# Who issues the transfers: weight and row loads from SyncE instead of GpSimd, stores from ScalarE

## The chip, the cores and the metric

The kernel runs on one core of a Trainium2 chip. The metric is the time of one execution on the device in microseconds (us), median of three runs. The core has TensorE (PE), VectorE (DVE), ScalarE (ACT), GpSimd (POOL) and SyncE (SP), and 16 DMA engines that move data between the chip's memory (HBM) and the on-chip memory.

## What is computed

For each of 128 samples the kernel adds to `x` (64 x 256, float32) its product with one of 64 weight matrices (256 x 256), chosen by the sample's category, and that category's bias:

```python
selected_W = W[cat_ids]
selected_b = b[cat_ids]
out = x + jnp.einsum('bsd,bdh->bsh', x, selected_W) + selected_b[:, None, :]
```

`x` is 8.4 MB, the result as much, a weight matrix 256 KB. With these inputs 54 of the 64 categories occur.

## The kernel before

**Plan.** From the categories the kernel first works out, on DVE and PE, a list of the categories in order of first use, so that each weight matrix is loaded once, into place n of `w_all`; "load n" below is the n-th of this list (0 to 63, of which 54 to 63 don't occur and are skipped by a condition). The list lies in `load_words`, four 6-bit categories to a 32-bit word; the issuing engine reads a word and takes a category out of it with shifts (`words_read` L162, `part` L166). A second list, `slot_words`, tells for each sample the place of its weights.

**Groups.** Samples are handled in 16 groups of 8, a group being four pairs. Rows of a group (512 KB) are loaded into one of ten slots of `rows` (`load_rows` L178). For each group PE transposes the rows of the *next* group (`transpose_half` L462, L464), writes the bias sums (L538), and does four pairs of products (L552). The weights of a sample are copied from `w_all` to `w_slot`, of even samples by DVE and of odd ones by ACT (`copy_weights` L298, L304); a copy waits until as many loads are reported as its place needs (L303), and until the pair that used the slot is done. ACT also copies the transposed rows from PSUM (`x_half` L309, L316). DVE adds the sums to the rows in place (`add_rows` L432, L433), two pairs at a time, and in groups 1 to 3 splits the bias (L419 to L427). Then the rows are stored.

Group 0 needs loads 0 to 7, group 1 up to 13, group 2 up to 19, group 3 up to 25, group 4 up to 31, and so on with fewer new ones: group 5 up to 32, 6 up to 37, 7 up to 40, 8 up to 43, 9 up to 46, 10 up to 47, 11 up to 51, 12 to 14 up to 52, 15 up to 53.

**Who issues what.** SyncE loads the categories, rows 0 to 2 and the bias, then loads 1, 3, 5, 7; ACT loads 0, 2, 4, 6. After that SyncE only reports: it waits for each load in order and adds one to `w_loads_done` (L211 to L217). GpSimd issues loads 8 to 63 (L260 to L279, `load_weights` L169, L170), beginning when three loads are reported (L263), with at most eight of them in flight (L274). Behind fixed loads it also issues the rows of groups 3 to 15 (`X_AFTER_LOAD` L37, L285) and the stores of groups 0 to 6 (`STORE_AFTER_LOAD` L38, L288); rows of group 10 and up wait until the store that frees their slot has landed. After the last load it stores groups 7 to 10 (L289). SyncE stores groups 11 to 14 in halves (L183) and two pairs of group 15 (L191), ACT the other two.

Transfers issued by GpSimd run on a queue that the profile calls software_dynamic (q0); those of SyncE and ACT on hardware_dynamic ones (q1 and q10).

Of the kernel before, what the change touches and what calls it, by code (L numbers as in the profile page):

```python
# [12 lines left out]
GROUP = 8  # L13
QUAD = 4
# [5 lines left out]
LOADS_IN_FLIGHT = 8  # L20
FIRST_X = 3
FIRST_LOADS = 8
REPORTED_FIRST = 3
CERTAIN_LOADS = 40
# [10 lines left out]


X_AFTER_LOAD = {3: 13, 4: 19, 5: 25, 6: 31, 7: 33, 8: 37, 9: 40, 10: 43, 11: 46, 12: 48, 13: 51, 14: 55, 15: 60}  # L37
STORE_AFTER_LOAD = {0: 37, 1: 40, 2: 43, 3: 46, 4: 48, 5: 51, 6: 59}  # L38
POOL_GROUPS = 11


def build_cond_residual(nc, x, cat, weights, bias, out):
# [18 lines left out]
    assert FIRST_LOADS % WORD == 0  # L61
    assert all(at + 1 >= min(C, GROUP * (g + 1) + QUAD - 1) for g, at in STORE_AFTER_LOAD.items())
    assert all(X_AFTER_LOAD[g + X_SLOTS] >= STORE_AFTER_LOAD[g] for g in range(GROUPS - X_SLOTS))

# [5 lines left out]
    with ExitStack() as ctx:  # L70
# [91 lines left out]
        def words_read(engine, words, most):  # L162

            return nc.values_load_multi_w_load_instructions(words, engines=[engine], min_val=0, max_val=most)[1]  # L164

        def part(word, n):  # L166
            return (word >> (BITS * n)) & (C - 1)

# [9 lines left out]
        def load_rows(engine, g):  # L178
            engine.dma_start(rows[:, g % X_SLOTS, :, :], x_groups[g]).then_inc(x_loaded[g], 16)  # L179
# [6 lines left out]
        def store_group(engine, g):  # L186
            engine.dma_start(out_groups[g], rows[:, g % X_SLOTS, :, :]).then_inc(stored[g % X_SLOTS], 16)  # L187
# [8 lines left out]
        @block.sync  # L196
        def _(sp):
            sp.dma_start(cats_i[:, :], cat.rearrange("(a b) -> a b", a=1)).then_inc(cats_loaded, 16)
            load_rows(sp, 0)
            sp.dma_start(bias_nat[:, :], bias).then_inc(bias_loaded, 16)  # L200
            for g in range(1, FIRST_X):
                load_rows(sp, g)

            sp.wait_ge(plan_read, 1)
            for n in range(1, FIRST_LOADS, PAIR):
                if n % WORD == 1:

                    word = words_read(mybir.EngineType.SP, load_words[0:1, n // WORD:n // WORD + 1],
                                      2 ** (WORD * BITS) - 1)[0]
                load_weights(sp, n, part(word, n % WORD))  # L210
            for n in range(C):  # L211

                if n < FIRST_LOADS:
                    sp.wait_ge(first_w_loaded[n], 16)
                else:
                    sp.wait_ge(w_loaded[n % LOADS_IN_FLIGHT], 16 * ((n - FIRST_LOADS) // LOADS_IN_FLIGHT + 1))
                sp.sem_inc(w_loads_done, 1)  # L217
            for q in range(QUADS_IN_GROUP * POOL_GROUPS, last_group):

                sp.wait_ge(sums_added, q + 1)  # L220
                store_quad(sp, q, late_stored)
            for p in range(0, PAIRS_IN_GROUP, PAIR):

                sp.wait_ge(sums_added, last_group + p + 1)
                store_pair(sp, p, last_stored)

            for g in range(POOL_GROUPS - X_SLOTS, POOL_GROUPS):
                sp.wait_ge(stored[g % X_SLOTS], stores_until(g))
            sp.wait_ge(late_stored, 16 * (last_group - QUADS_IN_GROUP * POOL_GROUPS))
            sp.wait_ge(last_stored, 16 * PAIRS_IN_GROUP)  # L230

        @block.gpsimd
        def _(pool):
# [16 lines left out]
                      allow_small_or_imprecise_dtypes=True).then_inc(consts_ready, 1)  # L250
            def store_sums(g):

                pool.wait_ge(sums_added, QUADS_IN_GROUP * (g + 1))
                store_group(pool, g)

            def list_word(w):
                return words_read(mybir.EngineType.Pool, load_words[0:1, w:w + 1], 2 ** (WORD * BITS) - 1)[0]


            pool.wait_ge(plan_read, 1)  # L260
            word = list_word(FIRST_LOADS // WORD)

            pool.wait_ge(w_loads_done, REPORTED_FIRST)  # L263
            for n in range(FIRST_LOADS, C):
                if n % WORD == 0 and n > FIRST_LOADS:
                    word = next_word
                if n % WORD == WORD - 1 and n + 1 < C:

                    next_word = list_word(n // WORD + 1)
                if n == CERTAIN_LOADS:  # L270
                    loads = words_read(mybir.EngineType.Pool, load_words[0:1, LIST_WORDS:LIST_WORDS + 1], C)[0]
                if n >= FIRST_LOADS + LOADS_IN_FLIGHT:

                    pool.wait_ge(w_loads_done, n - LOADS_IN_FLIGHT + 1)  # L274
                if n >= CERTAIN_LOADS:

                    load_weights(pool, n, part(word, n % WORD), cond=loads > n)
                else:
                    load_weights(pool, n, part(word, n % WORD))  # L279
                for g, after in X_AFTER_LOAD.items():  # L280
                    if after == n:
                        if g >= X_SLOTS:

                            pool.wait_ge(stored[g % X_SLOTS], stores_until(g - X_SLOTS))
                        load_rows(pool, g)  # L285
                for g, after in STORE_AFTER_LOAD.items():
                    if after == n:
                        store_sums(g)  # L288
            for g in range(len(STORE_AFTER_LOAD), POOL_GROUPS):  # L289
                store_sums(g)  # L290

# [16 lines left out]
        def _(act):  # L308
# [14 lines left out]
            act.wait_ge(cats_loaded, 16)  # L323
            load_weights(act, 0, words_read(mybir.EngineType.Activation, cats_i[0:1, 0:1], C - 1)[0])

            act.wait_ge(plan_read, 1)
# [10 lines left out]
            for g in range(GROUPS):  # L337
                if g >= 1:
                    for k in range(K):
                        x_half(g, k)  # L340

                now = slots
                if g + 1 < GROUPS:
                    slots = slots_of(mybir.EngineType.Activation, g + 1, 1)
                for p in range(PAIRS_IN_GROUP):
                    copy_weights(act, nc.scalar.copy, now[p], g, p, 1, odd_weights_ready)
            for p in range(1, PAIRS_IN_GROUP, PAIR):

                act.wait_ge(sums_added, last_group + p + 1)
                store_pair(act, p, last_stored)  # L350
# [108 lines left out]
        def _(pe):  # L459
# [22 lines left out]
            for n in range(WORD):  # L482
                T.matmul(load_words_ps, cat_powers[:, n:n + 1], has_place[:, n::WORD],
                         start=(n == 0), stop=(n == WORD - 1))
            T.matmul(loads_ps, is_first[:, :], ones[:, :], start=True, stop=True).then_inc(plan_products, 1)
            pe.wait_ge(plan_step, PLAN_STEPS["slots"])
            for n in range(WORD):
# [8 lines left out]

            pe.wait_ge(x_loaded[0], 16)
            for k in range(K):
                transpose_half(0, k)
            def group(g):  # L500
# [79 lines left out]
```

## Time and profile before

| | |
|---|---|
| median of three runs | 101.41 us (101.09 to 101.49) |
| the profiled execution | 101.62 us |
| its span (first to last record) | 99.9 us |
| granted TensorE clock, mean | 0.997 of full |
| busy: PE, DVE, ACT, POOL | 88%, 58%, 56%, 54% |
| moved by DMA | 31.19 MB, mean 312 GB/s |

All times inside the execution are counted from the span's start. The time of an execution holds the span and 1.7 us around it. A transfer's landing is when its semaphore is complete; loads count as available to the copies when SyncE has reported them.

### The profile page before, as it was taken

The page shows a single profiled execution, that of the slowest core. Times are in us where ns is not written, and L with a number is a line of the kernel's source. Part 1 is how long each engine was busy: PE and PEld are TensorE (multiplying, and loading weights), DVE is VectorE, ACT ScalarE, POOL GpSimd, SP SyncE. Part 2 cuts the span into 40 slices and gives each one's busy share as a digit, 9 for nine tenths or more (in the row PEclk, how much of TensorE's full clock was granted, in tenths as well). Part 3 has the DMA queues.
Part 4 walks back from the last instruction along what each step waited for, and adds up shares of the span by engine and source line. Part 5 has one row for each costly group of instructions (what it writes and reads, how often), then busy time and mean ns, then how long its engine had stood idle before and what let it go on. Part 6 is the DMA issues. An engine that isn't in the chain of part 4 may idle for free.

```text
span 99.9 us, 3043 instructions
## 1 busy us (share of the span) xinstructions
PE 87.6 (88%) x788; PEld 58.0 (58%) x788; DVE 58.4 (58%) x139; ACT 55.7 (56%) x98; POOL 53.8 (54%) x91
## 2 busy tenths in 40 slices
PE   0279559995699999899999999999999999999990
PEld 0148336753366667476767676666676767676640
DVE  2757126415989688864747484847373737373840
ACT  6004239363263565697848484858585858585500
POOL 5100088798799799988858755794333650000000
PEclk9999999999999999999999999999999999999998
DMA  0899988899999999999999999999998899993363
GB/s 0 268 322 366 349 223 285 297 298 362 318 323 354 354 353 336 354 348 346 390 374 390 366 397 372 398 387 385 380 369 300 272 337 337 343 302 105 105 210 108
DMA packets 13747, 31.19 MB, mean 312 GB/s; under 512 B 1505, under 2 KB 7714, under 8 KB 13730
## 3 DMA queue, kind: packets, MB, share of 16 engines
q0 software_dynamic: 7136, 24.65, 69.9%
q1 hardware_dynamic: 5218, 5.05, 15.4%
q10 hardware_dynamic: 1376, 1.31, 3.9%
q8 instruction: 6, 0.10, 0.4%
q14 instruction: 11, 0.09, 0.3%
HBM read 25.23 MB, written 8.39 MB: 336 GB/s over the span
## 4 chain that ended last, share of the span: by engine, by line
PE 56%; DMA 26%; issue 7%; POOL 2%; DVE 2%; POOLq 2%; SPq 1%; ACT 1%; ACTq 0%; DVEq 0%
PE mm_ps L552 37%; DMA w_all<-in_L_cond_W 25%; PE xt_ps L464 10%; PE mm_ps L538 6%; POOL w_all L170 2%; PE xt_ps L552 2%; DMA cats_i<-in_itok_B 1%; POOLq L170 1%; POOLq L164 1%; SPq L164 1%; ACT w_slot L304 1%; DVE rows L433 0%; POOL rows L179 0%; DVE same_ahead L381 0%; PE mm_ps L476 0%
## 5 line engine op out<-in xcount | busy, mean ns | idle before, releaser
L552 PE MATMUL mm_ps<-w_slot,xT 128*64 128x256 f32 x496 | 57.6, 380 | 3.7 <-DVE w_slot L304 1.9
L304 ACT COPY w_slot<-w_all 128x512 f32 x64 | 38.7, 619 | 31.7 <-SPq L217 20.9
L552 PEld LDWEIGHTS mm_ps<-w_slot,xT 128*64 128x64 f32 x496 | 34.4, 137 | 21.4 <-DVE w_slot L304 5.5
L170 POOL DMA_DIRECT2D w_all<-in_L_cond_W x56 | 33.8, 606 | 20.7 <-SPq L217 13.4
L433 DVE TENSOR_TENSOR rows<-mm_ps,rows 128x512 f32<-128x512 f32 (+1 forms) x32 | 21.5, 673 | 22.9 <-PE mm_ps L552 22.6
L304 DVE COPY w_slot<-w_all 128x512 f32 x64 | 27.7, 463 | 10.2 <-SPq L217 10.1
L316 ACT COPY xT<-xt_ps 128x512 f32<-128x512 f32 x32 | 17.2, 584 | 5.9 <-PE xt_ps L464 5.9
L464 PE MATMUL xt_ps<-ident,rows 128*128 128x128 f32 x128 | 19.1, 298 | 0.0
L464 PEld LDWEIGHTS xt_ps<-ident,rows 128*128 128x128 f32 x128 | 15.1, 151 | 6.4 <-issue 5.3
L179 POOL DMA_DIRECT2D rows<-in_x x13 | 10.1, 780 | 4.7 <-DMA out<-rows 3.3
L538 PE MATMUL mm_ps<-bias_parts,is_sample 96*64 96x256 bf16 x124 | 9.9, 278 | 0.0
L187 POOL DMA_DIRECT2D out<-rows x11 | 8.4, 769 | 1.1 <-issue 0.6
L538 PEld LDWEIGHTS mm_ps<-bias_parts,is_sample 96*64 96x64 bf16 x124 | 5.6, 109 | 3.3 <-issue 3.2
L470 PE MATMUL mm_ps<-bias_nat,in_category 64*96 64x256 f32 x8 | 3.1, 479 | 1.2 <-DVE rows L433 1.0
L422 DVE CAST bias_parts<-mm_ps 96x256 bf16<-96x256 f32 x4 | 1.7, 420 | 2.1 <-PE mm_ps L470 1.2
L476 PE MATMUL mm_ps<-cats,ones_row 1*128 1x128 bf16 x1 | 0.3, 283 | 2.7 <-DVE cats L373 2.7
L470 PEld LDWEIGHTS mm_ps<-bias_nat,in_category 64*96 64x96 f32 x8 | 1.1, 182 | 1.9 <-issue 1.5
L552 PE MATMUL xt_ps<-w_slot,xT 128*64 128x256 f32 x16 | 2.1, 379 | 0.0
L321 ACT ACT_TABLE_LOAD x1 | 1.3, 1283 | 0.9 <-PEq L569 0.9
L423 DVE TENSOR_TENSOR bias_rest<-mm_ps,bias_parts 96x256 f32<-96x256 f32 x4 | 1.7, 420 | 0.1
L426 DVE TENSOR_TENSOR bias_parts<-bias_rest,bias_mid 32x256 bf16<-32x256 f32 x4 | 1.7, 417 | 0.1
L476 PEld LDWEIGHTS mm_ps<-cats,ones_row 1*128 1x128 bf16 x1 | 0.1, 99 | 2.7 <-DVE cats L373 2.7
(46 smaller groups left out, 13.2 us busy)
## 6 DMA issues: line engine op xcount, KB each, us to landing
w_all<-in_L_cond_W POOLq DMA_DIRECT2D x56, 256.0 KB
rows<-in_x POOLq DMA_DIRECT2D x13, 512.0 KB, 7.0
out<-rows POOLq DMA_DIRECT2D x11, 512.0 KB, 7.6
out<-rows SPq DMA_DIRECT2D x8, 256.0 KB, 3.7
rows<-in_x SPq DMA_DIRECT2D x3, 512.0 KB, 6.5
w_all<-in_L_cond_W ACTq DMA_DIRECT2D x4, 256.0 KB, 5.7
w_all<-in_L_cond_W SPq DMA_DIRECT2D x4, 256.0 KB, 6.4
out<-rows SPq DMA_DIRECT2D x2, 128.0 KB, 1.7
```

Source lines behind the costliest of these rows:

```text
L164: return nc.values_load_multi_w_load_instructions(words, engines=[engine], min_val=0, max_val=most)[1]
L170: engine.dma_start(w_all[:, n, :, :], weights[bass.ds(c, 1), :, :].rearrange("c (k p) h -> p (c k) h", p=P), **how).then_inc(first_w_loade ...
L179: engine.dma_start(rows[:, g % X_SLOTS, :, :], x_groups[g]).then_inc(x_loaded[g], 16)
L187: engine.dma_start(out_groups[g], rows[:, g % X_SLOTS, :, :]).then_inc(stored[g % X_SLOTS], 16)
L304: copy(w_slot[:, PAIR * p + half, :, :].rearrange("p k h -> p (k h)"), w_all[:, bass.ds(c, 1), :, :].rearrange("p c k h -> p (c k h)")).th ...
L316: nc.scalar.copy(xT[:, slot, k].rearrange("p j s -> p (j s)"), xt_ps[slot][k][:, :, :].rearrange("p t r -> p (t r)")).then_inc(xT_ready, 1)
L422: split(V.tensor_copy(bias_parts[all3, t, :], whole))
L433: V.tensor_tensor(to, sums, to, ALU.add).then_inc(sums_added, 1)
L464: last = T.transpose(xt_ps[g % XT_SLOTS][k][:, p, :], rows[:, g % X_SLOTS, p, k * P:(k + 1) * P], ident[:, :])
L470: return T.matmul(bias_ps[t], in_category[:, t, :, :].rearrange("c a n -> c (a n)"), bias_nat[:, :], start=True, stop=True)
L538: T.matmul(sums(pair)[HALF * half:HALF * (half + 1), :], is_sample[:, sample + half:sample + half + 1].broadcast_to([ROWS, HALF]), bias_pa ...
L552: last = T.matmul(to[HALF * half:HALF * (half + 1), :], xT[:, slot, k, j, :], w_slot[:, j, k, :], start=False, stop=(k == K - 1), skip_gro ...
```

## The change

SyncE issues loads 8 to 63 right behind its own first ones, and the rows of groups 1 and 3 to 15; it reads each word of the list when it needs it. GpSimd, after making its constants, only reports. ACT issues rows 2 behind load 0, and stores groups 0 to 9, each behind its copies of a fixed later group (`STORED_IN_GROUP`); it has a wait for the sums first, of groups whose sums are older. Group 10 is now stored by SyncE in halves. In the first stage PE transposes group 0's rows before it packs the slot words, and ACT copies group 1's transposed rows between its first weight copies. The rows of groups 11, 13, 14 and 15 are issued after a later load than before.

```diff
-FIRST_X = 3
-REPORTED_FIRST = 3
-X_AFTER_LOAD = {3: 13, 4: 19, 5: 25, 6: 31, 7: 33, 8: 37, 9: 40, 10: 43, 11: 46, 12: 48, 13: 51, 14: 55, 15: 60}
-STORE_AFTER_LOAD = {0: 37, 1: 40, 2: 43, 3: 46, 4: 48, 5: 51, 6: 59}
-POOL_GROUPS = 11
+X_AFTER_LOAD = {3: 13, 4: 19, 5: 25, 6: 31, 7: 33, 8: 37, 9: 40, 10: 43, 11: 47, 12: 48, 13: 55, 14: 63, 15: 63}
+STORED_IN_GROUP = {0: 4, 1: 5, 2: 5, 3: 6, 4: 7, 5: 7, 6: 8, 7: 9, 8: 10, 9: 11}
...
-            return (word >> (BITS * n)) & (C - 1)
+            return (word >> (BITS * n)) & (C - 1) if n else word & (C - 1)
...
@@ sync
-            for g in range(1, FIRST_X):
-                load_rows(sp, g)
+            load_rows(sp, 1)
...
-            for n in range(C):
-
-                if n < FIRST_LOADS:
-                    sp.wait_ge(first_w_loaded[n], 16)
+            for n in range(FIRST_LOADS, C):
+                if n % WORD == 0:
+                    word = words_read(mybir.EngineType.SP, load_words[0:1, n // WORD:n // WORD + 1],
+                                      2 ** (WORD * BITS) - 1)[0]
+                if n == CERTAIN_LOADS:
+                    loads = words_read(mybir.EngineType.SP, load_words[0:1, LIST_WORDS:LIST_WORDS + 1], C)[0]
+                if n >= FIRST_LOADS + LOADS_IN_FLIGHT:
+
+                    sp.wait_ge(w_loads_done, n - LOADS_IN_FLIGHT + 1)
+                if n >= CERTAIN_LOADS:
+
+                    load_weights(sp, n, part(word, n % WORD), cond=loads > n)
                 else:
-                    sp.wait_ge(w_loaded[n % LOADS_IN_FLIGHT], 16 * ((n - FIRST_LOADS) // LOADS_IN_FLIGHT + 1))
-                sp.sem_inc(w_loads_done, 1)
-            for q in range(QUADS_IN_GROUP * POOL_GROUPS, last_group):
+                    load_weights(sp, n, part(word, n % WORD))
+                for g, after in X_AFTER_LOAD.items():
+                    if after == n:
+                        if g >= X_SLOTS:
+
+                            sp.wait_ge(stored[g % X_SLOTS], stores_until(g - X_SLOTS))
+                        load_rows(sp, g)
+            for q in range(QUADS_IN_GROUP * ACT_GROUPS, last_group):
...
@@ gpsimd
...
+            for n in range(C):
+
+                if n < FIRST_LOADS:
+                    pool.wait_ge(first_w_loaded[n], 16)
                 else:
-                    load_weights(pool, n, part(word, n % WORD))
...
+                    pool.wait_ge(w_loaded[n % LOADS_IN_FLIGHT], 16 * ((n - FIRST_LOADS) // LOADS_IN_FLIGHT + 1))
+                pool.sem_inc(w_loads_done, 1)
@@ scalar
             load_weights(act, 0, words_read(mybir.EngineType.Activation, cats_i[0:1, 0:1], C - 1)[0])
+            load_rows(act, 2)
...
-                if g >= 1:
+                if g >= XT_SLOTS:
                     for k in range(K):
                         x_half(g, k)
...
                     copy_weights(act, nc.scalar.copy, now[p], g, p, 1, odd_weights_ready)
+                    if g == 0 and p < K:
+
+                        x_half(1, p)
+                for s, at in STORED_IN_GROUP.items():
+                    if at == g:
+
+                        act.wait_ge(sums_added, QUADS_IN_GROUP * (s + 1))
+                        store_group(act, s)
@@ tensor
             T.matmul(loads_ps, is_first[:, :], ones[:, :], start=True, stop=True).then_inc(plan_products, 1)
+
+            pe.wait_ge(x_loaded[0], 16)
+            for k in range(K):
+                transpose_half(0, k)
             pe.wait_ge(plan_step, PLAN_STEPS["slots"])
...
             bias_of_tile(0).then_inc(plan_products, 1)
 
-            pe.wait_ge(x_loaded[0], 16)
-            for k in range(K):
-                transpose_half(0, k)
```

## Rows read from the trace of the kernel before

**Rows 1.** The page: span, busy time, and DMA in 40 slices of 2.5 us
```profile
span 99.9 us, 3043 instructions
...
PE 87.6 (88%) x788; PEld 58.0 (58%) x788; DVE 58.4 (58%) x139; ACT 55.7 (56%) x98; POOL 53.8 (54%) x91
...
DMA  0899988899999999999999999999998899993363
GB/s 0 268 322 366 349 223 285 297 298 362 318 323 354 354 353 336 354 348 346 390 374 390 366 397 372 398 387 385 380 369 300 272 337 337 343 302 105 105 210 108
```

**Rows 2.** The chain in order of time, from 34 us: start us, us, what
```profile
34.78 6.20 DMA w_all<-in_L_cond_W
...
41.11 0.63 ACT w_slot L304
41.74 0.14 issue
41.88 1.08 PE mm_ps L552 x8
42.96 1.02 PE xt_ps L464 x8
...
78.21 1.02 PE xt_ps L464 x8
...
83.25 1.02 PE xt_ps L464 x8
...
97.26 0.42 DVE rows L433
```

**Rows 3.** Windows: length, busy us (count) of each engine, clock, DMA share, GB/s
```profile
core 0: us, PE busy (x) PEld busy (x) DVE busy (x) ACT busy (x) POOL busy (x), PEclk, DMA share, GB/s
12.73:41.88 29.15, 25.78 (x223) 16.19 (x223) 19.51 (x43) 15.28 (x28) 26.08 (x36) 1.00 0.96 321
65.00:70.00 5.00, 5.00 (x52) 3.40 (x50) 2.90 (x6) 3.41 (x7) 3.40 (x7) 1.00 1.03 387
```

**Rows 4.** Windows, by stages of the transfers
```profile
7.50:10.00 2.50, 2.50 (x12) 2.15 (x11) 1.80 (x6) 1.17 (x2) 0.00 (x0) 1.00 1.08 367
8.00:9.00 1.00, 1.00 (x6) 0.66 (x5) 0.92 (x3) 0.59 (x1) 0.00 (x0) 1.00 1.08 377
10.00:12.50 2.50, 1.38 (x13) 0.84 (x11) 0.48 (x2) 0.53 (x1) 0.00 (x0) 1.00 1.09 349
12.50:15.00 2.50, 1.43 (x12) 0.90 (x14) 0.70 (x2) 0.85 (x3) 2.20 (x3) 1.00 0.83 222
20.00:30.00 10.00, 7.94 (x70) 4.78 (x68) 6.32 (x16) 4.88 (x10) 8.99 (x13) 1.00 0.94 325
30.00:41.00 11.00, 10.95 (x102) 7.14 (x100) 8.90 (x20) 5.67 (x11) 10.03 (x15) 1.00 1.03 351
41.00:75.00 34.00, 33.59 (x321) 22.70 (x319) 21.25 (x42) 24.91 (x45) 22.95 (x37) 1.00 1.02 376
```

**Rows 5.** Waits of GpSimd, and its timeline at the first load it issues
```profile
POOL w_all L170 <- SPq L217: 13.4, 8, 10.0
...
12.80 2.31 POOL L170 DMA_DIRECT2D w_all<-in_L_cond_W  x3 [10.04 <-SPq L217]
```

**Rows 6.** Line 217, SyncE's reports, counted up to 15.46, 41.01 and 75.46 us
```profile
L217 SPq EVENT_SEMAPHORE  x8: 17/17/17, 9.5 to 15.4; - x8
...
L217 SPq EVENT_SEMAPHORE  x32: 17/17/17, 9.5 to 41.0; - x32
...
L217 SPq EVENT_SEMAPHORE  x54: 17/17/17, 9.5 to 75.4; - x54
```

**Rows 7.** SyncE's timeline of its loads, and line 179 on SyncE (rows 0)
```profile
6.84 0.54 SPq L170 DMA_DIRECT2D w_all<-in_L_cond_W  x1
...
8.31 0.39 SPq L170 DMA_DIRECT2D w_all<-in_L_cond_W  x1
...
9.04 0.38 SPq L170 DMA_DIRECT2D w_all<-in_L_cond_W  x1
...
L179 SPq DMA_DIRECT2D rows<-in_x x3: 429/507/577, 1.3 to 3.0; - x3
...
DMA to landing us min/median/max: 3.6/6.5/7.3
```

**Rows 8.** Line 187, GpSimd's stores between 42 and 67 us
```profile
L187 POOL DMA_DIRECT2D out<-rows x6: 757/757/787, 42.4 to 66.3; - x6
```

**Rows 9.** The page's DMA queues: packets, MB, share of 16 engines
```profile
q0 software_dynamic: 7136, 24.65, 69.9%
q1 hardware_dynamic: 5218, 5.05, 15.4%
```

**Rows 10.** GpSimd's timeline: the last skipped loads
```profile
76.54 0.04 POOL L170 DMA_DIRECT2D w_all<-in_L_cond_W  x1
77.12 0.04 POOL L170 DMA_DIRECT2D w_all<-in_L_cond_W  x1 [0.32 <-issue]
77.71 0.04 POOL L170 DMA_DIRECT2D w_all<-in_L_cond_W  x1 [0.54 <-SPq L217]
```

More of the change, by code:

```diff
@@ L61, in build_cond_residual @@
     assert FIRST_LOADS % WORD == 0
-    assert all(at + 1 >= min(C, GROUP * (g + 1) + QUAD - 1) for g, at in STORE_AFTER_LOAD.items())
-    assert all(X_AFTER_LOAD[g + X_SLOTS] >= STORE_AFTER_LOAD[g] for g in range(GROUPS - X_SLOTS))
+    ACT_GROUPS = len(STORED_IN_GROUP)
+    assert all(g < at for g, at in STORED_IN_GROUP.items())
+    assert all(X_AFTER_LOAD[g + X_SLOTS] + 1 >= min(C, GROUP * (STORED_IN_GROUP[g] + 1))
+               for g in range(GROUPS - X_SLOTS))
     x_groups = x.rearrange("(g p h) s d -> g (h s) p d", p=PAIRS_IN_GROUP, h=PAIR)
@@ L225, in _ @@
                 store_pair(sp, p, last_stored)
-            for g in range(POOL_GROUPS - X_SLOTS, POOL_GROUPS):
+            for g in range(ACT_GROUPS - X_SLOTS, ACT_GROUPS):
                 sp.wait_ge(stored[g % X_SLOTS], stores_until(g))
-            sp.wait_ge(late_stored, 16 * (last_group - QUADS_IN_GROUP * POOL_GROUPS))
+            sp.wait_ge(late_stored, 16 * (last_group - QUADS_IN_GROUP * ACT_GROUPS))
             sp.wait_ge(last_stored, 16 * PAIRS_IN_GROUP)
@@ L250, in _ @@
                       allow_small_or_imprecise_dtypes=True).then_inc(consts_ready, 1)
[L251 to L277, printed above, removed]
-                else:
-                    load_weights(pool, n, part(word, n % WORD))
[L280 to L290, printed above, removed]
+            for n in range(C):
+                if n < FIRST_LOADS:
+                    pool.wait_ge(first_w_loaded[n], 16)
+                else:
+                    pool.wait_ge(w_loaded[n % LOADS_IN_FLIGHT], 16 * ((n - FIRST_LOADS) // LOADS_IN_FLIGHT + 1))
+                pool.sem_inc(w_loads_done, 1)
         def slots_of(engine, g, half):
```

## The prediction

> The sum is made against the profiled execution: span 99.9 us and 1.7 us around it, 101.6 us in all, which is 0.2 us above the median of the three runs (101.41). The forecast is given against the median.
>
> **What bounds the kernel now.** The page comes first [rows 1]: no engine is full over the whole span, and the DMA engines are near full from the second slice to the thirtieth. So the chain is read next, in order of time [rows 2]. It has two parts. Up to 41.9 us it runs through weight loads: load 31 is issued at 34.78, lands at 40.97, ScalarE copies it at 41.11, and group 4's last pair starts at 41.88. From 42.96 on every group follows the last at 5.04 us with no gap, on TensorE alone (group 5 at 42.96, group 12 at 78.21), down to the last sum at 97.26. So the end moves by what the start of group 5 moves, as long as nothing later makes a group wait. In the first part TensorE idles 3.4 us between its first pair and group 4's last [rows 3], 29.15 less 25.78; more than about that can't be won there.
>
> Then the transfers, by stage [rows 4]. The first eight loads and rows 0 to 2 run at 367 and 349 GB/s, on the hardware queues of SyncE and ScalarE (358 together). Then comes a hole: 222 GB/s from 12.5 to 15, 325 from 20 to 30, and only from 30 on 351. The waits say why [rows 5]: GpSimd sits 10.0 us and issues load 8 at 12.80, since it waits for three reported loads. From 41 to 75 the transfers are full again, at 376 GB/s with stores among them.
>
> The landings, counted by SyncE's reports, are the measure for all that follows [rows 6]: load 7 at 15.4, load 31 at 41.0, load 53 (the last; the inputs hold 54 categories) at 75.4.
>
> **The first part after the change.** SyncE goes on to load 8 right behind load 7. Its issues stand at 6.84, 8.31 and 9.04 [rows 7]: 0.73 us for a load, and 1.47 where a word of the list is read between, so a word costs 0.74; a rows issue costs 0.5 and some 0.1 around it. Load 8 then goes out at about 9.04 + 1.4 = 10.4, 2.4 us before GpSimd's. Six loads, one and a half words and one rows issue are 4.4 + 1.1 + 0.6 = 6.1 us for 2.10 MB, 344 GB/s; the shift spared at every fourth load brings some 0.1 back, 350 GB/s. That is barely the pace of the transfers, but SyncE starts with the first stage's backlog ahead of it (3.74 MB issued by 9.4, of which 268 x 2.5 + 322 x 2.5 + 366 x 1.9 = 2.2 MB had moved [rows 1]), so the DMA engines stay full. Between load 7's and load 31's landing lie 24 loads and rows 3 to 5, 7.86 MB. They took 25.6 us, 307 GB/s. At full pace, which I put at 355, between the software queue's 351 and the hardware queues' 358, they take 22.1, and load 31 lands at 37.5. Gain 3.5, cut to TensorE's 3.4. From below: if the transfers only reach the 325 of 20 to 30 us, it is 24.2 us and a gain of 1.4.
>
> Other edits of this stage go at nothing. Rows 2 behind load 0 on ScalarE's queue moves the same bytes before load 7. The earlier transposes of group 0, and group 1's copies between group 0's, lie before or beside waits for loads: the first pair starts only at 12.73. GpSimd does nothing but report; a report is 17 ns on SyncE [rows 6], its own wake-up is not shown, 0 to 0.1 us, once. Without that cover each of these would cost 0.5 us or so.
>
> **The middle, where the gain is at stake.** Two things change. First, stores come earlier. GpSimd issues only stores 0 to 5 before load 53's landing, the sixth of them at 66.27 [rows 8]. ScalarE issues store 0 after group 4's copies, 1 and 2 after group 5's, 3 after 6, 4 and 5 after 7, and one each after 8 to 11. Its copies of a group end some 0.6 us after TensorE starts it, so stores 0 to 8 are wholly ahead of rows 13, and store 9 (issued some 4 us before rows 13 are wanted) about two thirds: 9.65 stores. Rows 13 themselves now follow load 53.
>
> Second, a store changes its price. Between load 31 and load 53 lie 22 loads and 8 rows, 9.96 MB, and 6 stores, in 34.4 us. Loads alone would take 9.96 / 0.351 = 28.4, so a store, 0.52 MB, adds only 1.0 us: stores overlap with loads. After the change stores ride on hardware queues. Their packets are a quarter in size: 5.05 MB in 5218 packets on q1, 24.65 MB in 7136 on q0, and a MB takes 3.05% of the DMA engines' span against 2.84% [rows 9]. Whether such a queue overlaps as well is what the trace can't say; the most that two hardware queues moved was 377 GB/s, at 8 to 9 us [rows 4], and those were loads alone. If 377 is their ceiling and a store takes half of it, it lasts 2.78 us, in which loads move 0.52 MB and not 0.99: 1.3 us for a store. From below 1.0 as now, from above 0.52 / 0.355 = 1.5, no overlap at all. I take 1.3.
>
> Rows 13 then land at 37.5 + 9.96 / 0.355 + 9.65 x 1.3 = 37.5 + 28.1 + 12.5 = 78.1. TensorE wants them at the start of group 12, which would be 78.21 - 3.4 = 74.8. It waits 3.3 us (in part earlier, at rows 8 and 10 and at load 46, which have the same queues before them), and of the 3.4 won 0.1 is left.
>
> The Trainium skill (DMA: Bandwidth & Descriptors, "Issuing engines are not separate DMA queues") says that transfers started by SyncE, ScalarE or GpSimd run on the same 16 engines, and that another issuer saves only sequencer time. By it a store would go on costing 1.0 and the sum would be that of the first rival below. No run here shows yet which holds. The same page ("Queues, rings and completion order") has each engine take turns between queues, which is why a store may take half.
>
> **The end.** SyncE issues rows 14 and 15 only after iteration 63, and the last three skipped ones wait for load 53's report; GpSimd spends 0.6 us on such an iteration (76.54, 77.12, 77.71) [rows 10]. Rows 13 landing at 78.1, load 53 at 76.6, rows 14 go out at about 78.5 and land 3.6 us later when nothing is ahead of them (rows 0 [rows 7]), 6.5 at the median: 82.1 to 85.0. They are wanted at 83.25. I take 0.2 us for it, bounds 0 and 1.8. ScalarE's ten issues of 0.4 us each lie in its idle time: it is busy 3.4 of 5 us in the second window of [rows 3]; its wait for the sums is for sums two groups old and never lasts. Uncovered they would be 4 us. The last stores are issued as before.
>
> **Sum:** -3.4 + 3.3 + 0.2 = +0.1 us: 101.7 against the profiled execution's 101.6, 101.5 against the median.
>
> **The rivals.**
> - Stores overlap on hardware queues as they do now, 1.0 us each. Rows 13 land at 37.5 + 28.1 + 9.65 = 75.3, half a microsecond late; the gain is 2.9 and the time 98.5. For it: all transfers use the same engines, and the limit of loads (351) is visibly not that of the engines (376 with stores). Against: the smaller packets. Stores of 1.15 give 1.5 of gain, 99.9. Chance 0.35 for this side.
> - No overlap, 1.5 us a store: rows 13 at 37.5 + 28.1 + 14.5 = 80.1, 5.3 us late, 1.9 of them beyond the gain: 103.3. It is slower than before from a price of about 1.35 on. For it: loads alone already fill the share at 1.08 and 1.09 in the hardware stage [rows 4], so there may be no room for more. Chance 0.26.
> - The start isn't won whole, because SyncE with its inline word reads issues no faster than the transfers run, and any wait starves them. Load 31 at 39.6, and all later landings 2.1 us later: 103.6. Its point: SyncE's six loads and rows taking over 6 us. Chance 0.12.
> - The forecast, won at the start and given back in the middle, within 0.5%: 0.27.
>
> **How the numbers follow.** 0.5%, about 0.5 us, is what a measurement of this kernel can tell from no change. Faster is the first rival, 0.35. Slower is the second and third, 0.38. Within 0.5% is left with 0.27. The far ends are 98.0 (all of the 3.4 held) and over 105 (a start at 325 GB/s and stores at 1.5 together). I leave a tenth out at each side: 99.0 to 103.7. Since both signs hold most of the chance: the forecast's own range, with stores at 1.25 to 1.35, is 101.0 to 102.0.
>
> **What the new profile would show.** First part: no hole at 12.5 to 30 us, load 31's report at 37 to 38, group 5 starting at 39.6. Middle: hardware queues alone, 365 to 380 GB/s from 41 to 75, and waits of TensorE for rows of groups 8, 10, 11 or 13 or for copies in groups 6 to 9, some 3 us in all. ScalarE's stores without waits. If instead 385 GB/s and no wait stand there, the first rival holds; if 350 and 5 us of waits, the second. If load 31 lands at 39.5 with the DMA share below 1, it is the third. It would all be wrong if the middle were not full of transfers, or if TensorE waited for anything but loads.

## The result and the profile after

The changed kernel takes 102.16 us at the median of 20 runs (101.64 to 103.9), the kernel before, measured beside it, 101.49 (100.87 to 103.06). The ratio is 1.0065, with a 95% interval of 1.0042 to 1.0088: slower by two thirds of a per cent. The two profiled executions lie closer together, 101.78 and 101.62 us, with spans of 100.0 and 99.9; so what follows explains why nothing was gained, and of the 0.67 us between the medians the traces show only 0.16.

The page of the changed kernel, to be read beside [rows 1, 9]:

```profile
span 100.0 us, 3042 instructions
...
PE 89.9 (90%) x788; PEld 60.1 (60%) x788; DVE 56.2 (56%) x139; ACT 54.9 (55%) x98; POOL 1.7 (2%) x11
...
DMA  0899999999999999999999999999998279953363
GB/s 10 259 319 358 352 348 348 350 353 356 347 348 348 348 348 352 359 384 376 385 384 378 372 369 386 385 390 370 382 372 300 63 238 339 384 184 111 108 210 105
DMA packets 31811, 31.19 MB, mean 312 GB/s; under 512 B 1521, under 2 KB 31794, under 8 KB 31794
...
q1 hardware_dynamic: 24610, 23.93, 72.8%
q10 hardware_dynamic: 7184, 7.08, 20.4%
```

GpSimd has gone from 54% to 2% busy. The hole between 12.5 and 30 us (223 to 323 GB/s in all slices but one) is filled, 347 to 356 throughout. The packets went from 13,747 to 31,811 for the same bytes, and yet the middle moves as much as before. The windows say the same, against [rows 4]:

```profile
core 0: us, PE busy (x) PEld busy (x) DVE busy (x) ACT busy (x) POOL busy (x), PEclk, DMA share, GB/s
...
12.50:15.00 2.50, 2.48 (x12) 1.59 (x14) 0.56 (x2) 1.79 (x4) 0.00 (x0) 1.00 1.10 348
...
20.00:30.00 10.00, 10.00 (x92) 6.22 (x91) 8.25 (x20) 5.29 (x10) 0.00 (x0) 1.00 1.10 351
30.00:41.00 11.00, 11.00 (x103) 7.43 (x102) 7.75 (x18) 7.08 (x14) 0.00 (x0) 1.00 1.10 349
41.00:75.00 34.00, 32.25 (x308) 22.26 (x307) 18.19 (x39) 20.36 (x38) 0.00 (x0) 1.00 1.09 379
```

The reports, now by GpSimd, counted up to 15.40, 38.46 and 65.85 us, answer to [rows 6]:

```profile
L268 POOLq EVENT_SEMAPHORE  x8: 17/17/17, 8.0 to 15.4; - x8
...
L268 POOLq EVENT_SEMAPHORE  x32: 17/17/17, 8.0 to 38.4; - x32
...
L268 POOLq EVENT_SEMAPHORE  x48: 17/17/17, 8.0 to 65.8; - x48
```

Load 31 is reported at 38.4, 2.6 us before its time in the kernel before. TensorE's timeline shows what became of that (start us, us, and in brackets the idle time before and who ended it):

```profile
40.67 1.09 PE L451 MATMUL xt_ps<-ident,rows 128*128 128x128 f32 x8
...
51.14 1.09 PE L451 MATMUL xt_ps<-ident,rows 128*128 128x128 f32 x8 [0.32 <-DMA rows<-in_x]
...
55.72 1.08 PE L540 MATMUL mm_ps<-w_slot,xT 128*64 128x256 f32 x8 [0.34 <-DVE w_slot L282]
56.73 1.09 PE L451 MATMUL xt_ps<-ident,rows 128*128 128x128 f32 x8
...
68.12 1.09 PE L451 MATMUL xt_ps<-ident,rows 128*128 128x128 f32 x8 [1.09 <-DMA rows<-in_x]
...
78.20 1.09 PE L451 MATMUL xt_ps<-ident,rows 128*128 128x128 f32 x8
```

The same view of the kernel before, for groups 5 and 12 (the chain of [rows 2] counts both 0.07 us later):

```profile
42.89 1.09 PE L464 MATMUL xt_ps<-ident,rows 128*128 128x128 f32 x8
...
78.14 1.09 PE L464 MATMUL xt_ps<-ident,rows 128*128 128x128 f32 x8
```

The first line of each is the start of group 5: it comes 2.2 us earlier than before. At 5.04 us a group, group 10 would start at 65.87. It starts at 68.12: TensorE waited for rows 8 before group 7, for a weight inside group 7, and for rows 11 before group 10 (and 0.2 us more in small gaps inside group 8). That is 2.25 us, all of the gain, and from there on both kernels keep the same pace; group 12 starts at 78.20 here and at 78.14 there.

### The profile page after: what moved, and what is told of

It is laid out like the page before. It is cut to its first block, busy times and chain, and to the rows that moved or that the text cites. A ratio compares the mean times of both kernels' runs of the same rounds, so it can differ in the third digit from the quotient of the medians.

```text
span 100.0 us, 3042 instructions
## 1 busy us (share of the span) xinstructions
PE 89.9 (90%) x788; PEld 60.1 (60%) x788; DVE 56.2 (56%) x139; ACT 54.9 (55%) x98; POOL 1.7 (2%) x11
## 2 busy tenths in 40 slices
DMA packets 31811, 31.19 MB, mean 312 GB/s; under 512 B 1521, under 2 KB 31794, under 8 KB 31794
## 4 chain that ended last, share of the span: by engine, by line
PE 30%; DMA 29%; SPq 27%; issue 7%; DVE 2%; ACT 1%; ACTq 0%; POOLq 0%; DVEq 0%
PE mm_ps L540 19%; DMA w_all<-in_L_cond_W 19%; SPq L169 18%; DMA rows<-in_x 11%; PE xt_ps L451 5%; SPq L178 5%; SPq L163 4%; PE mm_ps L526 3%; PE xt_ps L540 2%; ACT L299 1%; DVE rows L420 0%; DVE same_ahead L368 0%; ACTq L163 0%; DVE has_place L380 0%; PE mm_ps L463 0%
## 5 line engine op out<-in xcount | busy, mean ns | idle before, releaser
L540 PE MATMUL mm_ps<-w_slot,xT 128*64 128x256 f32 x496 | 59.3, 392 | 0.9 <-ACT w_slot L282 0.5
L282 ACT COPY w_slot<-w_all 128x512 f32 x64 | 37.8, 620 | 31.7 <-POOLq L268 24.2
L540 PEld LDWEIGHTS mm_ps<-w_slot,xT 128*64 128x64 f32 x496 | 36.3, 142 | 18.6 <-DVE w_slot L282 1.9
L282 DVE COPY w_slot<-w_all 128x512 f32 x64 | 25.6, 422 | 12.0 <-POOLq L268 11.7
L540 PEld LDWEIGHTS xt_ps<-w_slot,xT 128*64 128x64 f32 x16 | 1.1, 137 | 0.6
L420 DVE TENSOR_TENSOR rows<-xt_ps,rows 128x256 f32<-128x256 f32 x2 | 0.8, 424 | 0.9 <-PE xt_ps L540 0.9
L412 DVE CAST bias_parts<-bias_rest 32x256 bf16<-32x256 f32 x4 | 1.1, 284 | 0.1
```

What stands on the lines that cost most here:

```text
L282: copy(w_slot[:, PAIR * p + half, :, :].rearrange("p k h -> p (k h)"), w_all[:, bass.ds(c, 1), :, :].rearrange("p c k h -> p (c k h)")).th ...
L420: V.tensor_tensor(to, sums, to, ALU.add).then_inc(sums_added, 1)
L540: last = T.matmul(to[HALF * half:HALF * (half + 1), :], xT[:, slot, k, j, :], w_slot[:, j, k, :], start=False, stop=(k == K - 1), skip_gro ...
```

## The experiments

Ten runs, in three sets. The ratio is always to the kernel before, timed on the same chip in the same set; what counts between two runs of different sets is therefore the ratio.

**All ten stores late.** ScalarE issues them about when the kernel before did. The assertion that guards other inputs against a deadlock is left out, so this one is for the experiment only.

```diff
-STORED_IN_GROUP = {0: 4, 1: 5, 2: 5, 3: 6, 4: 7, 5: 7, 6: 8, 7: 9, 8: 10, 9: 11}
+STORED_IN_GROUP = {0: 5, 1: 6, 2: 7, 3: 8, 4: 9, 5: 10, 6: 12, 7: 13, 8: 13, 9: 14}
...
-    assert all(X_AFTER_LOAD[g + X_SLOTS] + 1 >= min(C, GROUP * (STORED_IN_GROUP[g] + 1))
-               for g in range(GROUPS - X_SLOTS))
```

> The changed kernel with its ten stores issued by ScalarE as late as the kernel before issued them (behind groups 5 to 10 and 12 to 14 instead of 4 to 11). Theory 1 (the early stores give the start's gain back): four stores and not seven are ahead of rows 11, at 1.2 to 1.3 us each, so rows 11 land near 64.5 and TensorE runs without a wait from group 1 on: group 10 starts near 65.9 instead of 68.1, span 97.8, time 2 to 2.3 us under the changed kernel, about 99.3, faster than before by 2%. Theory 2 (the hardware queue itself is too slow for loads and stores together): rows 11 still land after 67, time within 0.7 us of the changed kernel.

Measured: 99.29 us, ratio 0.9765 (0.9708 to 0.9822), and once more in the third set 99.51, 0.9783 (0.9739 to 0.9827), for which stood:

> The run with all ten stores late once more, for a sharper number beside the one with eleven slots: 99.3, ratio 0.975 to 0.98. If eleven slots do what theory 1 says, the two differ by less than 0.5 us.

In the trace of the first, TensorE has no wait from group 1 on (groups 7 to 10 are shown):

```profile
50.48 1.09 PE L449 MATMUL xt_ps<-ident,rows 128*128 128x128 f32 x8
55.52 1.09 PE L449 MATMUL xt_ps<-ident,rows 128*128 128x128 f32 x8
60.55 1.09 PE L449 MATMUL xt_ps<-ident,rows 128*128 128x128 f32 x8
65.59 1.09 PE L449 MATMUL xt_ps<-ident,rows 128*128 128x128 f32 x8
```

Group 10 starts at 65.59 and not 68.12. In the second trace it starts at 65.93; there groups 3 to 5 start 0.2 to 1.0 us late, for weight loads, and no later group waits. Nothing was changed but when the stores go out: the queues, the packets and the loads are those of the changed kernel, and so is the later place of rows 11. So the change with its stores late is worth some 2.3% (the two intervals together reach from 1.7 to 2.9), and the early stores take it all back. Theory 2, that a hardware queue is too slow for both, has fallen.

**How many early stores.** The same line alone, with all its assertions, in two steps. Four early:

```diff
+STORED_IN_GROUP = {0: 4, 1: 5, 2: 5, 3: 6, 4: 9, 5: 10, 6: 12, 7: 13, 8: 13, 9: 14}
```

> The changed kernel with one line edited: stores 0 to 3 stay behind ScalarE's groups 4, 5, 5, 6, and stores 4 to 9 go behind groups 9, 10, 12, 13, 13, 14 instead of 7, 7, 8, 9, 10, 11; all its assertions hold. Theory 1 (each store ahead of rows 11 costs them 1.2 to 1.5 us, and groups 7 to 10 wait for that): four stores are ahead of rows 11 instead of seven, these land near 64, before group 10 is due at 65.9, though rows 8 may still be 0.3 us late; time 99.3 to 99.8, a ratio to before near 0.98. Rival (in the run with all ten late it was stores 0 to 3, which take from the last loads of group 5 to 7, that mattered): group 10 still starts after 67.5 and the ratio is above 0.995.

Five early:

```diff
+STORED_IN_GROUP = {0: 4, 1: 5, 2: 5, 3: 6, 4: 8, 5: 9, 6: 10, 7: 11, 8: 12, 9: 13}
```

> The same line with a smaller move: stores 4 to 9 behind groups 8 to 13. One more store (4, issued near 56) is ahead of rows 11 than in the run with four, and part of store 5. Theory 1: rows 11 land 1.2 to 1.8 us later than there, near 65.5 to 66, about when group 10 is due; time 99.5 to 100.5, between the two. Rival: a threshold and no price for each store; the time is that of one of the two neighbours.

Measured: 100.45 us, 0.9924 (0.9883 to 0.9966), and 100.66 us, 0.9953 (0.9901 to 1.0006). For four I had written 99.3 to 99.8, so this is 0.7 us more than that. The two can't be told apart in time; in the landings they can. Below are the reports counted to load 31 and to load 47, and the issue of rows 11 with its time to landing, which is what group 10 waits for. First the run with four early stores (its last two lines are for rows 11 and 12 together; rows 11 are the first, with 7.7 us):

```profile
L268 POOLq EVENT_SEMAPHORE  x32: 17/17/17, 7.8 to 38.7; - x32
...
L268 POOLq EVENT_SEMAPHORE  x48: 17/17/17, 7.8 to 63.2; - x48
...
L178 SPq DMA_DIRECT2D rows<-in_x x2: 507/606/705, 57.0 to 58.9; - x2
...
DMA to landing us min/median/max: 7.7/7.8/7.9
```

Then the run with five:

```profile
L268 POOLq EVENT_SEMAPHORE  x32: 17/17/17, 8.3 to 38.2; - x32
...
L268 POOLq EVENT_SEMAPHORE  x48: 17/17/17, 8.3 to 64.2; - x48
...
L178 SPq DMA_DIRECT2D rows<-in_x x1: 461/461/461, 57.1 to 57.1; - x1
...
DMA to landing us min/median/max: 8.7/8.7/8.7
```

And rows 11 in the changed kernel, with seven:

```profile
L178 SPq DMA_DIRECT2D rows<-in_x x1: 806/806/806, 57.2 to 57.2; - x1
...
DMA to landing us min/median/max: 10.9/10.9/10.9
```

From load 31 to load 47 it takes 24.5 us with four stores ahead, 26.0 with five and 27.4 with seven (the changed kernel): 2.9 us for three stores, 1.0 us each. To the landing of rows 11 it takes 25.9, 27.6 and 29.6 us: 3.7 us for three stores, 1.2 each. So a store costs 1.0 to 1.2 us, near the 1.0 that the prediction worked out for the software queue from [rows 4, 6], and somewhat over it for the landing that decides. With five, rows 11 land at 65.8, before group 10 starts at 67.0, so the fifth store costs TensorE nothing; what delays that run is a wait of 1.0 us for rows 8. Why four were not as good as ten late ones stands in the timeline of the run with four:

```profile
50.83 1.09 PE L451 MATMUL xt_ps<-ident,rows 128*128 128x128 f32 x8
...
55.76 1.08 PE L540 MATMUL mm_ps<-w_slot,xT 128*64 128x256 f32 x8 [0.69 <-ACT w_slot L282]
56.78 1.09 PE L451 MATMUL xt_ps<-ident,rows 128*128 128x128 f32 x8
```

Group 8 starts at 56.78, as in the changed kernel (56.73), since stores 0 to 2 are ahead of rows 8 and load 40 in both. From there on it has no wait. So the stores cost in two places: 0 to 2 in groups 6 and 7, and 4 to 6 at group 10.

**Eleven row slots.** With one slot more, all assertions hold with later stores. Against the run with four early stores, stores 0 and 2 go a group later and store 3 two groups; store 1 stays behind group 5, and 4 to 9 stay too.

```diff
-X_SLOTS = 10
+X_SLOTS = 11
...
+STORED_IN_GROUP = {0: 5, 1: 5, 2: 6, 3: 8, 4: 9, 5: 10, 6: 12, 7: 13, 8: 13, 9: 14}
...
-            for g in range(ACT_GROUPS - X_SLOTS, ACT_GROUPS):
+            for g in range(max(0, ACT_GROUPS - X_SLOTS), ACT_GROUPS):
```

> The changed kernel with eleven row slots instead of ten, and the stores behind groups 5, 5, 6, 8, 9, 10, 12, 13, 13, 14; the eleventh slot lets all its assertions hold with stores 0 to 2 a group later. Theory 1: what was left in the run with four early stores was the wait for rows 8 at 50.8 us and for the last weights of group 7 at 55.8, 1.1 us together, behind stores 0 to 2. With stores 0 and 1 near 41.5 and store 2 near 46.5, one and a half stores fewer are ahead of rows 8: no wait there, group 10 starts 0.6 to 1.1 us earlier than there, time 99.3 to 99.9, ratio to before about 0.98. Rival: those waits come from the loads' own pace after group 5, and the time stays at 100.4.

Measured: 99.71 us, 0.9788 (0.9748 to 0.9828), 0.2 us from all ten late. The waits at rows 8 and inside group 7 are gone (group 7 starts at 51.19, group 8 at 56.23, 5.04 apart). This one beats both kernels, by 2.1% and some 2.7%, and keeps the assertions that guard other inputs, as the changed kernel does. As store 3 moved as well, the run doesn't show what each of the three stores gave.

**Stores by GpSimd.** About the same times (most of the ten go out 0.5 to 2.6 us later), but on the software queue. GpSimd issues a store behind a fixed report; the guard is left out again.

```diff
+STORED_AFTER_REPORT = {0: 31, 1: 33, 2: 33, 3: 36, 4: 40, 5: 40, 6: 43, 7: 46, 8: 47, 9: 53}
...
-                for s, at in STORED_IN_GROUP.items():
-                    if at == g:
-
-                        act.wait_ge(sums_added, QUADS_IN_GROUP * (s + 1))
-                        store_group(act, s)
...
                 pool.sem_inc(w_loads_done, 1)
+                for s, at in STORED_AFTER_REPORT.items():
+                    if at == n:
+                        pool.wait_ge(sums_added, QUADS_IN_GROUP * (s + 1))
+                        store_group(pool, s)
```

> The changed kernel with stores 0 to 9 issued by GpSimd, between its reports, at about the times at which ScalarE issued them. Theory 1 (it is the number of stores ahead, at nearly one price on either queue): rows 11 land within 1 us of 68.1 and the time stays within 0.7 us of the changed kernel. Theory 2 (stores are dear because of the hardware queue's small packets): a store costs 1.0 us as in the kernel before and not 1.3, seven are ahead of rows 11, so these land 2 us earlier, near 66, and the time is 1.5 to 2 us lower, about 100.

Measured: 103.05 us, 1.0128 (1.0074 to 1.0183). Theory 1 holds: larger packets didn't make stores cheaper. With the same seven stores ahead, load 47 is reported 27.4 us behind load 31 in both kernels, and rows 11 land at 68.13, against 68.08. The software queue is if anything worse, by 0.6% on the changed kernel. Its group 10 starts at 68.18, against 68.12, and it loses more later, before group 13, at rows 14:

```profile
84.59 1.09 PE L449 MATMUL xt_ps<-ident,rows 128*128 128x128 f32 x8 [0.99 <-DMA rows<-in_x]
```

That is the wait that the prediction priced at 0.2 us, bounds 0 and 1.8. The Trainium skill (DMA: Bandwidth & Descriptors, "Issuing engines are not separate DMA queues"), by which the issuer saves only sequencer time, agrees with these two measurements on the price of a store. It doesn't cover the next two runs, where the queue mattered.

**The start alone.** The kernel before, whose GpSimd no longer waits for three reports:

```diff
-            pool.wait_ge(w_loads_done, REPORTED_FIRST)
```

> The kernel before, but GpSimd issues load 8 as soon as it has the first word and doesn't wait for three reports. Theory 1 (the hole after the first stage is what the change fills): GpSimd issues load 8 near 6 us; if its queue shares fairly with the others, load 31 is reported 2 to 3 us earlier, near 38.5, and the time falls to about 99.5. Rival: the software queue's 4 KB packets take the DMA engines from the first eight loads, which are the ones that TensorE waits for: load 1 and 3 are reported 2 us or more later than 11.8 and 13.8, groups 0 and 1 start later, and the time is 100.5 to 102.

Measured: 107.65 us, 1.0547 (1.0445 to 1.0648), far above either expectation. GpSimd does issue load 8 at 6.56. But the landings of SyncE's four first loads, line 170 on SP, went from 5.7/6.4/6.9 us in the kernel before to

```profile
DMA to landing us min/median/max: 8.1/12.5/14.3
```

and the reports, counted up to 18.2 and 23.7 us, are these:

```profile
L217 SPq EVENT_SEMAPHORE  x5: 17/17/17, 9.3 to 18.1; - x5
...
L217 SPq EVENT_SEMAPHORE  x16: 17/17/17, 9.3 to 23.6; - x16
```

Loads 8 to 15 had landed by the time load 7 did: eleven reports come within 1.8 us, the last nine 0.07 us apart. The last of these eight, load 15, was issued at 13.5 us, 4.7 us behind load 7, and yet landed no later: the software queue overtook the hardware ones, and what TensorE needed first came last. The engines were full meanwhile, at 356 GB/s from 10 to 20 us. TensorE waited three times, 2.94, 1.95 and 1.77 us, for group 0's weights, and its matmuls were slow as well, eight in 1.98 us where the kernel before has 1.08. Group 1 started at 26.30 and not at 17.50, and from there on TensorE had no wait, so that group 5 started 5.4 us late (48.32) and the end came 5.5 us late. Of this the last 16 slow matmuls of group 0, 3.68 us, are at most 1.7 (16 at 379 ns take 1.95 in the run with the old first stage); the rest are the late loads. So starting GpSimd at once doesn't fill the hole; SyncE's own queue does. A start behind one or two reports wasn't tried. The direction was the rival's; the size, 5 us and not 0.5, I had not thought possible. The Trainium skill (DMA: Bandwidth & Descriptors, "Queues, rings and completion order") says that an engine takes turns between queues a packet at a time. That fits: the mean packet of q0 is 3.6 times that of q1 [rows 9], so by an estimate from this rule, with one profiled packet to a turn, it gets 78% of the bytes beside one hardware queue and 64% beside two. The trace shows the landings, not the turns.

**Early stores on the kernel before.** Loads by GpSimd as before, ScalarE storing as in the changed kernel, SyncE storing group 10, guards left out:

```diff
-STORE_AFTER_LOAD = {0: 37, 1: 40, 2: 43, 3: 46, 4: 48, 5: 51, 6: 59}
-POOL_GROUPS = 11
+STORED_IN_GROUP = {0: 4, 1: 5, 2: 5, 3: 6, 4: 7, 5: 7, 6: 8, 7: 9, 8: 10, 9: 11}
+POOL_GROUPS = 10
```

> The kernel before, loads by GpSimd as they were, but ScalarE stores groups 0 to 9 behind the same groups as in the changed kernel, and SyncE stores group 10. Theory 1 (early stores take their share of the transfers wherever the loads come from): the kernel before had 2.5 to 3.3 us to spare in its middle, three more stores take 3 to 4.5 us of it; the time is 0.3 to 1.5 us above before. Rival (from the run in which GpSimd started at once: its 4 KB packets take several turns' worth of a hardware queue's 1 KB packets): the loads keep most of the engines, the stores wait, their landings take over 12 us instead of 8, and the time is within 0.3 us of before, unless a row slot comes free too late.

Measured: 103.36 us, 1.0169 (1.0054 to 1.0285), 1.7 us above before and so just past the upper end of theory 1; but the interval is wide, and its mechanism is neither theory's. The landings are the rival's. ScalarE's ten stores and the wait behind them, in the groups of instructions by source line:

```profile
L185 ACTq DMA_DIRECT2D out<-rows x10: 383/392/5134, 41.6 to 75.6; - x10
...
  POOL rows L177: 5.6, 2
...
DMA to landing us min/median/max: 7.7/14.6/19.9
```

A store takes 14.6 us to landing at the median, where the changed kernel has 8.2 and GpSimd's own stores took 7.6 in the kernel before (8.5 for the six that went out among the loads): GpSimd's loads, on the software queue, went ahead of ScalarE's stores. So row slots came free late, and GpSimd waited 5.6 us for two of them before it issued rows, 3.3 in the kernel before. To this comes something that neither theory had, in ScalarE's timeline:

```profile
53.85 5.56 ACTq L185 DMA_DIRECT2D out<-rows  x2
59.51 1.07 ACT L309 COPY xT<-xt_ps 128x512 f32<-128x512 f32 x2 [5.06 <-DVE rows L430]
```

Issuing the second of two stores took 5.1 us (its sums were older, so this is no wait for them), and behind it stood the copies of the rows that TensorE transposes in group 8. TensorE's timeline:

```profile
58.46 1.09 PE L461 MATMUL xt_ps<-ident,rows 128*128 128x128 f32 x8
60.64 0.63 PE L535 MATMUL mm_ps<-bias_parts,is_sample 96*64 96x256 bf16 x8 [1.08 <-ACT xT L309]
...
65.05 1.09 PE L461 MATMUL xt_ps<-ident,rows 128*128 128x128 f32 x8
```

Group 9 starts 6.6 us behind group 8 and not 5.04. That is 1.6 us of the 2.0 by which this trace is longer; the other 0.5 was lost before group 5 (43.35 against 42.89). No other group from 5 on starts late, and TensorE waits for no rows there, so the late slots cost nothing that this trace shows: the block did. The ScalarE issues that the prediction put at nothing are hidden only as long as an issue takes its 0.4 us; in the changed kernel the longest took 0.7.

**The first stage undone**, and **with four early stores TensorE's part of it undone.** The first puts group 0's transposes behind the bias tile, group 1's copies behind group 0's, and rows 2 on SyncE; the second only the transposes:

```diff
-            pe.wait_ge(x_loaded[0], 16)
-            for k in range(K):
-                transpose_half(0, k)
...
             bias_of_tile(0).then_inc(plan_products, 1)
+            pe.wait_ge(x_loaded[0], 16)
+            for k in range(K):
+                transpose_half(0, k)
```

> The changed kernel with the edits of its first stage undone: group 0's transposes behind the bias tile, group 1's ScalarE copies behind group 0's weights, rows 2 from SyncE. Theory: in the changed kernel TensorE stood still from about 8.0 to 9.0 us and its matmuls of group 0 then took 634 ns and not 380 until 17.7, so group 1 started at 18.74 instead of 17.50. With the old order group 1 starts near 17.5 and group 5 near 39.5 instead of 40.7. As rows 11 set group 10's start at 68.1 in the changed kernel, the end hardly moves: within 0.5 us. Rival: the slow first group is what costs, and the time falls by 1.2 us.

> The run with four early stores, and TensorE's transposes of group 0 again behind the first bias tile. With the stores out of the way TensorE sets the pace from group 1 on, so a start of group 1 at 17.5 instead of 18.6 should now count. Theory 1: matmuls of group 0 take 380 ns and not 634, group 5 starts near 39.6 if load 31 is reported by 37.6; 0.5 to 1.1 us faster than the run with four early stores. Rival: loads set groups 1 to 4 (in the run with the old first stage load 31 was reported at 39.1 and group 5 started at 41.0), and nothing is gained.

Measured: 102.46 us, 1.0056 (1.0019 to 1.0093), the changed kernel's ratio; and 100.72, 0.9947 (0.9906 to 0.9988), against 0.9924 with the new order. As to the end, the first run is what the theory said, no change, though its group 5 didn't start at the 39.5 that the theory gave (its profiled execution, 103.46 us, is also the slowest of its ten); in the second the rival holds, no gain. Why, the rows of group 0 show. The changed kernel's group 0, line 540 up to 17.6 us and after 18:

```profile
L540 PE MATMUL mm_ps<-w_slot,xT x24: 630/634/687, 12.5 to 17.3; 128*64 128x256 f32 x24
...
L540 PE MATMUL mm_ps<-w_slot,xT x8: 378/380/481, 17.7 to 18.4; 128*64 128x256 f32 x8
```

The same matmuls take 634 ns and then 380; the kernel before had 379 at the median for all 32. The views give a granted clock of 1.00 for both stretches, but for the first that is no measurement: the trace's records of the granted clock begin at 17.86 us, with full clock, the level of 2.4 GHz, and a stretch without a record counts as 1.00. In the kernel before they begin at 10.62, ahead of group 0, in the two runs with the old order at 11.29 and 10.93, in the run of the start alone at 26.52, and in each of these the matmuls get faster there. So the slow matmuls are those before the clock is recorded as full. Which level they had is not recorded; that they take 1.7 times as long points to the lower one, 1.2 GHz. Group 1 thus starts at 18.74 and not at 17.50. With the old order it was 17.55 and 17.52. But then group 4 waits for load 31 (in the second run 0.42 us at 39.71, ended by ScalarE's copy), and group 5 starts at 40.99 and 40.72, against 40.67 in the changed kernel: loads and TensorE are level there, and either alone is worth nothing.

## Why the prediction was right, and where not

The forecast was no change, 101.5, and the measured 102.16 lies within the range of 99.0 to 103.7, but a little above the half per cent that counts as no change and above the forecast's own 101.0 to 102.0; its cause, a start won and given back in the middle, is what the runs show.

**The first part.** The hole is filled, as forecast, and SyncE's issue pace is enough. Load 31 was to land at 37.5 and is reported at 38.4; the step that was mis-sized is the pace of 355 GB/s. The 7.86 MB took 23.1 us, 341 GB/s, though the windows show 348 to 351. The start of group 5 was won by 2.2 us, not 3.4: load 31 alone would have allowed some 2.6. The sum put the first stage's edits at nothing; there group 0's slow matmuls cost 1.2 us at group 1, but the runs with the old order show that load 31 sets nearly the same start of group 5.

**The price of a store.** Put at 1.3 us between 1.0 and 1.5, it is 1.0 to 1.2 by the differences between runs. Taken together, the seven stores ahead of rows 11 cost 1.25 each: 29.6 us less 20.9 for loads and rows alone at 351 GB/s (7.34 MB: loads 32 to 47 and rows 6 to 11); a little less, if the part of store 7 is counted that had moved by then. So the sum's 1.3 is a little high, and the first rival's 1.0 is too low for the landings that TensorE waited for. The ceiling of 377 GB/s on which the 1.3 rests held: the changed kernel moves 379 over 34 us, and packets of a quarter of the size cost nothing there. The software queue with seven stores ahead gives 28.8 less 20.9, 1.1 each. The 1.0 of the kernel before is for six stores among more loads.

**Where the early stores bite.** The sum held up rows 13 against group 12 and named rows 8, 10 and load 46 as the same wait seen earlier. Rows 13 landed at 77.8 (issued at 69.38, 8.4 us to landing), 78.1 was forecast, and group 12 starts at 78.20: this is nearly exact, but partly by luck, since errors cancel. Load 31 came 0.9 us later than in the sum, loads and rows took 0.3 longer, and the stores took 11.0 us and not 12.5 (nine of them and about half of the tenth, 1.1 to 1.2 each). And nobody waited for rows 13: the whole wait had come before. The one that decided was for rows 11, at group 10. By the sum's own price it is 38.4 + 20.9 + 7 x 1.3 = 68.4, and they landed at 68.1. Group 10 was due at 65.9. Seven stores delay them, where in the kernel before three stood ahead of rows 11 in GpSimd's queue; rows 11 also come one load later, but with the stores late that costs no wait. Had I written out each deadline and not the last one alone, this would have stood there. (GpSimd's seventh store goes out at 74.14 us, just ahead of load 53's landing and not behind it; it is too late to matter in the sum.)

**What was hidden.** ScalarE's issues were, with 0.38 to 0.70 us each; GpSimd's reports cost nothing visible. Rows 14, for which the sum had 0.2 us, landed at 82.8 and were not waited for in the changed kernel; group 13 starts 5.04 us behind group 12.

**The rivals.** Stores at 1.0 us were to give 98.5. The lowest reading of the price is that 1.0, and the time is 102.2. Even at 1.0 rows 11 would have landed at 66.3, 0.4 us late. With the stores moved away the kernel comes to 99.3 to 99.7. No overlap, the second, is out: 1.5 each would have had rows 11 at 69.8, and the middle would not have moved 379 GB/s. The third, a start not won whole, came true in its outcome for a third of the gain, but not in its mechanism: the DMA share stays at 1.10 from 12.5 to 41 us, so SyncE's issues didn't starve the transfers.

**What stays open.** Of the 0.67 us between the medians only 0.16 is seen between the two profiled executions. And why the clock rises late in group 0: TensorE idled from 8.0 to 9.0 us in the changed kernel. All seven traces with the new order have the slow matmuls (5.10 to 6.29 us for the 32), and of the five with the old order the kernel before and both runs with the old first stage have none of them. But they are also in the run of the start alone and in the run with early stores on the kernel before, whose first stages have the old order (the second needed 6.61 us for the same 32, and its trace has no record of the clock), so the order alone is not shown to be the cause. Nor is the loss the same each time: the kernel with all ten stores late, profiled twice, took 5.83 and 5.10 us for them and started group 1 at 18.48 and 17.28. The Trainium skill (TensorE: Matmul & The Clock Gate, "The HAM clock gate") says that the number of slow matmuls at a start changes from run to run; those two executions agree, with the first record of the full clock at 17.12 and 15.18 us.

## What to carry to other kernels

When transfers are the bound for a stretch, write down for each awaited transfer what is queued ahead of it and when it is due; moving a store of 512 KB earlier moves every load behind it later by 1.0 to 1.25 us here, even where ScalarE has the time to issue them. Fill an early hole from the queue whose transfers are needed first, not from another one with larger packets. And ask what a buffer slot more allows: here it let three stores wait, and the time went from 0.992 of the kernel before, the best with ten slots and all assertions, to 0.979. The slot without SyncE's loads wasn't tried.

## What was not expected of the hardware

- Loads issued by GpSimd beside loads on the hardware queues went ahead of them: landings of SyncE's four loads rose from a median of 6.4 to 12.5 us, and the kernel's time by 5.5%. ScalarE's stores beside such loads took 14.6 us to landing instead of 8.2.
- An issue on a hardware queue can block its engine: 5.1 us on ScalarE beside software-queue loads; on SyncE in the changed kernel up to 2.2 us (this line of its timeline has 2.12), against 0.38 in an empty stretch.

```profile
61.46 2.12 SPq L169 DMA_DIRECT2D w_all<-in_L_cond_W  x1
```

- Packets of 1 KB instead of up to 4 KB, 31,811 against 13,747 in number, moved 379 GB/s with stores among them, where the software queue moved 376.
- A granted clock of 1.00 in a view can stand for no record at all. In eleven of the twelve traces the first record, of the full clock, begins between 10.6 and 26.5 us, and TensorE's matmuls get 1.5 to 1.7 times as fast there; the twelfth trace has no record. The mean of 0.997 given for the kernel before counts its first 10.6 us as full for the same reason.
